# A fused two-layer adapter network on one core: the first round's mix and gates moved between the first adapter's folding and the others'

## The reference

```python
# layer 0: a 64x64 channel matrix per sample, then a dense product with a top-2 mixture of low-rank experts
y = jnp.einsum('bct,bcd->bdt', x, W_cond[condition])          # "mix"
base = jnp.einsum('bnd,od->bno', y, W_base) + b_base
top_p, top_i = jax.lax.top_k(softmax(y @ W_gate.T), 2)        # "gates", "routing"
h = jnp.einsum('bnd,erd->bner', y, A)                         # 8 experts of rank 16
x = x + base + einsum('bner,eor->bno', h * route_w, B)        # "delta"
# layer 1: each sample has one of 8 full matrices W1[adapter_ids], then low-rank heads
z = jnp.einsum('bsi,boi->bso', x, W1[adapter_ids])
scores = 8 * softmax(z @ Wr.T + br)
x = x + 2 * einsum('bshr,hor,bsh->bso', z @ A1, B1, scores)
```

## Time and profile before

| | value |
|---|---|
| median of three runs | 737.5 us |
| profiled execution | 738.8 us, of which its span is 737.1 us |
| TensorE (PE) busy | 719.6 us, 98% |
| weight loads (PEld) busy | 644.0 us, 87% |
| VectorE (DVE) busy | 335.2 us, 45% |
| ScalarE (ACT) busy | 114.0 us, 15% |
| GpSimd (POOL) busy | 58.0 us, 8% |
| moved by DMA | 156.24 MB, mean 212 GB/s |
| granted TensorE clock | 1.00 |

### The profile page before, as it was taken

How to read it: one execution, slowest core, us unless ns; L and a number is a source line. 1 busy time by engine, 2 the same in 40 slices (tenths; PEclk the granted TensorE clock), 3 DMA queues, 4 the chain that set the end, 5 groups by cost and what they waited for, 6 DMA issues and landing times.

```text
span 737.1 us, 12345 instructions
## 1 busy us (share of the span) xinstructions
PE 719.6 (98%) x4502; PEld 644.0 (87%) x4502; DVE 335.2 (45%) x887; ACT 114.0 (15%) x309; POOL 58.0 (8%) x115
## 2 busy tenths in 40 slices
PE   8999999999999999999999999999999999999996
PEld 8999887888888988898889888888889888988996
DVE  2000196235533654264534663464436543674644
ACT  2222300111111111112111111111111111120111
POOL 1222310000100010001000110001000100010100
PEclk9999999999999999999999999999999999999999
DMA  7899994145634775359526773387437751485552
GB/s 280 320 416 381 385 410 136 58 158 178 223 134 140 251 238 208 115 204 299 190 85 229 240 245 120 128 262 238 152 115 255 255 182 58 172 307 217 202 219 72
DMA packets 49457, 156.24 MB, mean 212 GB/s; under 512 B 8836, under 2 KB 26244, under 8 KB 39172
## 3 DMA queue, kind: packets, MB, share of 16 engines
q1 hardware_dynamic: 38466, 78.72, 30.0%
q0 software_dynamic: 9216, 71.31, 28.1%
q10 hardware_dynamic: 1730, 5.58, 1.9%
HBM read 133.24 MB, written 22.35 MB: 211 GB/s over the span
## 4 chain that ended last, share of the span: by engine, by line
PE 83%; issue 7%; DVE 5%; POOL 2%; DMA 2%; ACT 1%; POOLq 0%; ACTq 0%; DVEq 0%
PE base_ps L348 17%; PE base_ps L349 17%; PE base_ps L350 17%; PE mix_both L371 7%; PE out_ps L419 4%; PE low_ps L419 4%; PE mix_both L384 3%; DMA adapter<-folded 2%; POOL adapter L960 2%; PE base_ps L357 2%; PE out_ps L348 2%; PE out_ps L349 2%; PE out_ps L350 2%; DVE w_lo L700 1%; PE out_ps L384 1%
## 5 line engine op out<-in xcount | busy, mean ns | idle before, releaser
L348 PE MATMUL base_ps<-yT,w_hi 128*128 128x512 f32 (+1 forms) x576 | 214.7, 373 | 1.3 <-DVE xT L820 1.1
L350 PE MATMUL base_ps<-yT,w_hi 128*128 128x512 f32 (+1 forms) x576 | 211.4, 367 | 0.0
L349 PE MATMUL base_ps<-yT,w_lo 128*128 128x512 f32 (+1 forms) x576 | 211.4, 367 | 0.0
L704 DVE TENSOR_TENSOR yT<-mix_both,yT 128x512 fp32r<-128x512 f32 x64 | 44.3, 692 | 240.3 <-ACT yT L577 240.2
L348 PEld LDWEIGHTS base_ps<-yT,w_hi 128*128 128x128 f32 x576 | 108.5, 188 | 20.9 <-DVE xT L820 4.0
L350 PEld LDWEIGHTS base_ps<-yT,w_hi 128*128 128x128 f32 x576 | 108.4, 188 | 18.0
L349 PEld LDWEIGHTS base_ps<-yT,w_lo 128*128 128x128 f32 x576 | 108.6, 189 | 15.4
L357 PE MATMUL base_ps<-ag_raw,stage 128*128 128x136 f32 x640 | 75.2, 280 | 2.2 <-issue 1.2
L357 PEld LDWEIGHTS base_ps<-ag_raw,stage 128*128 128x128 f32 x640 | 74.5, 190 | 3.0 <-issue 2.3
L974 POOL DMA_DIRECT2D adapter<-folded x60 | 32.1, 534 | 568.7 <-PE low_ps L419 495.4
L716 DVE TENSOR_TENSOR x1T<-xT,x1T 128x256 fp32r<-128x256 f32 x120 | 45.4, 420 | 61.0 <-ACT x1T L584 61.0
(11 more groups left out here) (150 smaller groups left out, 740.8 us busy)
## 6 DMA issues: line engine op xcount, KB each, us to landing
adapter<-folded POOLq DMA_DIRECT2D x63, 1088.0 KB, 5.4
stage<-in_w SPq DMA_DIRECT2D x40, 512.0 KB, 7.9
x_rows<-in_x SPq DMA_DIRECT2D x32, 512.0 KB, 4.3
xT<-in_x_turned SPq DMA_DIRECT2D x16, 1024.0 KB, 6.3
out<-xT SPq DMA_DIRECT2D x28, 512.0 KB, 3.0
folded<-adapter ACTq DMA_DIRECT2D x10, 544.0 KB, 6.7
w_raw<-in_w SPq DMA_DIRECT2D x8, 256.0 KB, 7.7
w_raw<-in_w SPq DMA_DIRECT2D x4, 512.0 KB, 11.8
```

The source lines that it names most:

```text
L348: pe.matmul(dst, st_hi, mv_lo, start=start, stop=False, skip_group_check=True)
L349: pe.matmul(dst, st_lo, mv_hi, start=False, stop=False, skip_group_check=True)
L350: return pe.matmul(dst, st_hi, mv_hi, start=False, stop=stop, skip_group_check=True)
L704: dve.tensor_tensor(yT[:, 1, k, :], mix_ps[k % 2][:, :], yT[:, 0, k, :], ALU.subtract).then_inc(yT_lo_done, 1)
```

## The change

In the first round alone:

- **The mix's banks.** The mix uses four banks (`mix_ps[0]`, `mix_ps[1]`, `low_ps`, `out_ps`), and chunk k waits for the low half of chunk k-4. The gates' waits follow: tile 0 starts after five chunks, and from chunk 5 on, and for each further tile, there is a wait of its own.
- **Order on TensorE.** The mix and the gates stand between `fold(0)` and the loop of the other adapters. ScalarE's `yT_high` and its exponential, and VectorE's `copy_hg` and `routing`, move with them; on VectorE they now stand before the splits.
- **Order on SyncE.** x of round 0 and `g0` are loaded behind the first adapter's units and before the others'. The channel matrices of round 0 leave this queue.
- **GpSimd.** It issues the channel matrices of round 0, under a semaphore of their own, before `low_of_adapter(0)`, and splits g0 right behind `low_of_adapter(0)`.
- **The first unit** is loaded in two halves of 512 columns, each with its semaphore; the fold waits for the second half at its fifth piece.
- ScalarE's plain copy of a folded unit goes to `lg` and not to `hg`, since `hg` now holds the gates' sums of round 0 while other adapters are folded.

```diff
+        def mix_bank(q, r, k):
+            return hg_banks[k % 4] if isinstance(q, int) and r == 0 else mix_ps[k % 2]
...
             e = first_adapter(sp)
-            for c in range(KC):
+            piece = w1[bass.ds(KC * e, 1), :, :].rearrange("a p n -> (a p) n")
+            sp.dma_start(stage[:, 0, 0:T], piece[:, 0:T]).then_inc(first_landed, 16)
+            sp.dma_start(stage[:, 0, T:D], piece[:, T:D]).then_inc(unit_landed[0], 16)
+            for c in range(1, KC):
                 load_unit(e, c)
-            sp.wait_ge(const_set, 5)
             sp.wait_ge(small_landed, 48)
-            load_wc(0, 0)
             total = adapters_in_use(sp)
+            load_x(0, 0)
+            sp.dma_start(g_raw[:, :, 1, :], g0).then_inc(g_landed, 16)
             with sp.Fori(1, total) as n:
                 e = adapter_at(sp, n)
                 for c in range(KC):
                     sp.wait_ge(unit_done, KC * n + c + 1)
                     load_unit(e, c)
-            load_x(0, 0)
-            sp.dma_start(g_raw[:, :, 1, :], g0).then_inc(g_landed, 16)
...
                 for c in range(KC):
-                    pe.wait_ge(unit_landed[c], 16 * n + 16)
+                    if c == 0 and isinstance(n, int):
+                        pe.wait_ge(first_landed, 16)
+                    else:
+                        pe.wait_ge(unit_landed[c], 16 * n + 16)
                     pe.wait_ge(unit_copied, KC * n + c + 1)
                     for oc in range(KC):
+                        if c == 0 and oc == HALF and isinstance(n, int):
+                            pe.wait_ge(unit_landed[0], 16)
...
-                if k >= 2:
-                    pe.wait_ge(yT_lo_done, at(q, r, KC, k - 1))
+                banks = 4 if isinstance(q, int) and r == 0 else 2
+                if k >= banks:
+                    pe.wait_ge(yT_lo_done, at(q, r, KC, k - banks + 1))
...
-                        if t == 0 and k in (0, KC - 1):
+                        if t == 0 and isinstance(q, int) and r == 0:
+                            if k == 0 or k >= 5:
+                                pe.wait_ge(yT_lo_done, max(5, k + 1))
+                        elif t == 0 and k in (0, KC - 1):
...
+                        if t and k == 0 and isinstance(q, int) and r == 0:
+                            pe.wait_ge(yT_lo_done, 5 + t)
...
             fold(0)
+            for k in range(KC):
+                mix(0, 0, k)
+            pe.wait_ge(g_split, 1)
+            gates(0, 0)
             total = adapters_in_use(pe)
             with pe.Fori(1, total) as n:
                 fold(n)
             pe.wait_ge(unit_copied, KC * total + BANKS)
-            for k in range(KC):
-                mix(0, 0, k)
             iteration(0, 0, l1=False)
...
-                act.copy(hg[:, c % 4, :], base_ps[c % BANKS][:, 0:HG]).then_inc(unit_copied, 1)
+                act.copy(lg[:, c % 4, :], base_ps[c % BANKS][:, 0:HG]).then_inc(unit_copied, 1)
...
             take_adapter(0, e, False)
+            for k in range(KC):
+                yT_high(0, 0, k)
+            route_exp(0, 0)
             total = adapters_in_use(act)
...
             for k in range(KC):
                 yT_low(0, 0, k)
+            for t in range(TILES):
+                copy_hg(0, 0, t)
+            routing(0, 0)
             for k in range(KC):
                 split(w_hi[:, k, 0:T], w_lo[:, k, 0:T], w_raw[:, k, 0:T], w_landed[k], k)
...
+            pool.wait_ge(const_set, 5)
+            pool.wait_ge(small_landed, 48)
+            for i in range(PER):
+                no = pool.value_load(ids[0:1, i:i + 1], min_val=0, max_val=CONDS - 1)
+                half = slice((i % 2) * CH, (i % 2 + 1) * CH)
+                pool.dma_start(wc[half, i // 2, half], w_cond[bass.ds(no, 1), :, :].rearrange("a p n -> (a p) n")
+                               ).then_inc(first_wc_landed, 16)
             low_of_adapter(0)
+            pool.wait_ge(g_landed, 16)
+            pool.tensor_copy(g_hl[:, :, 0, :], g_raw[:, :, 1, :]).then_inc(g_split_hi, 1)
+            pool.wait_ge(g_split_hi, 1)
+            pool.tensor_tensor(g_hl[:, :, 1, :], g_raw[:, :, 1, :], g_hl[:, :, 0, :], ALU.subtract).then_inc(g_split, 1)
```

More of the change, by code:

```diff
@@ L154, in build @@
         ag1_landed = sem("ag1_landed")
+        first_landed = sem("first_landed")
         unit_landed = [sem(f"unit_landed{s}") for s in range(STAGE)]
@@ L173, in build @@
         wc_landed = sem("wc_landed")
+        first_wc_landed = sem("first_wc_landed")
         xT_landed = [sem(f"xT_landed{h}") for h in range(4)]
@@ L469, in iteration @@
                 first = isinstance(q, int) and r == 0
-                if first:
-                    pe.wait_ge(g_split, 1)
-                gates(q, r)
+                if not first:
+                    gates(q, r)
                 for k in range(KC):
@@ L576, in yT_high @@
                 act.wait_ge(yT_done, at(q, r, KC, k + 1))
-                act.copy(yT[:, 0, k, :], mix_ps[k % 2][:, :]).then_inc(yT_hi_done, 1)
+                act.copy(yT[:, 0, k, :], mix_bank(q, r, k)[:, :]).then_inc(yT_hi_done, 1)
             def x1T_high(q, r, i):
@@ L597, in lwT_high, with route_exp @@
                 act.copy(lwT[:, 0, toks], low_ps[:, toks]).then_inc(lwT_hi_done, 1)
+            def route_exp(q, r):
+                act.wait_ge(route_step, at(q, r, ROUTE_STEPS, 6))
+                act.activation(top_exp[:, :, :], top_d[:, :, :], ACT.Exp).then_inc(top_exp_done, 1)
             def iteration(q, r, l1=True, ahead=True):
@@ L602, in iteration @@
                     x1T_high(q, r - 1, 1)
-                act.wait_ge(route_step, at(q, r, ROUTE_STEPS, 6))
-                act.activation(top_exp[:, :, :], top_d[:, :, :], ACT.Exp).then_inc(top_exp_done, 1)
-                if l1:
+                    route_exp(q, r)
                     for i in range(2, PER):
@@ L626, in _ @@
                 take_adapter(n, e, True)
-            for k in range(KC):
-                yT_high(0, 0, k)
             iteration(0, 0, l1=False)
@@ L703, in yT_low @@
                 dve.wait_ge(yT_hi_done, at(q, r, KC, k + 1))
-                dve.tensor_tensor(yT[:, 1, k, :], mix_ps[k % 2][:, :], yT[:, 0, k, :], ALU.subtract
+                dve.tensor_tensor(yT[:, 1, k, :], mix_bank(q, r, k)[:, :], yT[:, 0, k, :], ALU.subtract
                                   ).then_inc(yT_lo_done, 1)
@@ L861, in iteration @@
             def iteration(q, r, l1=True, ahead=True, toks=ALL):
-                copy_hg(q, r, 0)
                 if l1:
+                    copy_hg(q, r, 0)
                     x1T_low(q, r - 1, 0)
-                copy_hg(q, r, 1)
-                if l1:
+                    copy_hg(q, r, 1)
                     x1T_low(q, r - 1, 1)
[L868 to L871, removed]
+                    copy_hg(q, r, 2)
+                    copy_hg(q, r, 3)
+                    routing(q, r)
                     for i in range(2, PER):
@@ L959, in low_of_adapter @@
                     pool.wait_ge(unit_copied, KC * n + c + 1 + BANKS)
-                    pool.tensor_tensor(adapter[:, 0, c, 1, :], hg[:, c % 4, :], adapter[:, 0, c, 0, :], ALU.subtract
+                    pool.tensor_tensor(adapter[:, 0, c, 1, :], lg[:, c % 4, :], adapter[:, 0, c, 0, :], ALU.subtract
                                        ).then_inc(folded_lo, 1)
+            pool.wait_ge(const_set, 5)
[5 more added lines that the diff above has]
+                               ).then_inc(first_wc_landed, 16)
             low_of_adapter(0)
+            pool.wait_ge(g_landed, 16)
+            pool.tensor_copy(g_hl[:, :, 0, :], g_raw[:, :, 1, :]).then_inc(g_split_hi, 1)
+            pool.wait_ge(g_split_hi, 1)
+            pool.tensor_tensor(g_hl[:, :, 1, :], g_raw[:, :, 1, :], g_hl[:, :, 0, :], ALU.subtract).then_inc(g_split, 1)
             total = adapters_in_use(pool)
```

10 lines of the change are left out of this document (4 added, 6 removed).

## The result

The changed kernel is slower by 0.5%: 741.86 us, median of 8 runs (740.01 to 743.27), against 738.27 us in 8 runs of the kernel before. The ratio is 1.0047, 95% interval 1.0036 to 1.0058. The forecast was 731.0, with 736.5 as its upper end. The profiled execution has a span of 741.2 us where before had 737.1.

A forecast was written before the change was run, and what follows sets the result against it. TensorE bounds the kernel, so only its idle time can be gained: base starts 5.2 us earlier and the 1.29 us routing wait goes, 6.5 us off the 737.5 median, giving 731.0 us; range 729.8 to 736.5.

The forecast's parts named there:

- The rival: Second round's channel matrices: SyncE's queue behaves as now, TensorE waits 11.6 us, 742.6 us in all; chance 0.10 (738 to 743).
- 40.3 us of queue against 28.7: From folds' end to second round's mix: matrices now take 40.3 us to arrive, the changed kernel wants them after 28.7.
- 27.2 us behind the folds' end: Second round's matrices: the queue shrinks, they land at 124.2 with folds ending at 97.0, 1.5 us before they are wanted.
- without b1 in front the first block of 11.5 us falls away: SyncE's issues of x's columns: the first blocked issue, 11.5 us, was held until b1 left the queue, so it goes.
- The margin: Second round's matrices land 1.5 us before wanted; chance of partly late 0.14 (732 to 736), of queue as now 0.10.
- The wait before the first mix: TensorE after the first fold: ready at 22.3, x lands at 22.8, so 0.5 us of wait, bounds 0 and 1.7.
- The first piece in two: Start of the first fold: half a unit lands earlier, 0.6 us gained, bounds 0 and 0.8; second unit may limit next.
- bound by loads: Rival in the fold loop: loads limit it, gain shrinks to 1 or 2 us, 736; chance 0.08 for little change.
- the 1.98 and the 1.29 us: TensorE idle before: 1.98 us at the second adapter's start, 1.29 us waiting for the routed rows; both were to go.
- hidden as put: First round's matrices on GpSimd's queue: landing near 20, hidden by the first fold, cost 0; upper bound 4.4 us.
- 97.6 predicted: Start of base on TensorE: 97.6 and not 102.9, 5.2 us gained.
- GpSimd beside VectorE's splits: Low parts of the last two adapters slow to 1.6 us at most against a unit's 1.85; folding keeps its pace.

## Why the prediction was wrong, point by point

**The rival had the mechanism, the forecast had the wrong size.** The text (731.0 us) put 40.3 us of queue against 28.7, and then let the queue shrink to 27.2 us behind the folds' end. It took 35.1 (folds' end 101.14, the mix started 136.25). Term by term: the store landed 6.6 us after its issue and not 5.0 (1.6). From its landing to the end of the last columns' issue were 15.6 us (109.0 to 124.63) and not 8.7 (6.9). The rest was 11.6 and not 12.3. **The step that failed is "without b1 in front the first block of 11.5 us falls away".** It became 7.0, and the second stayed at 5.9 us. b1 may have been a reason for the length of the first block, but it isn't one for there being a block. In the changed kernel b1 had landed by 109.5, no DMA was under way when the two x_turned were issued (the row below, in the order of the table by stretches), and still the third issue of columns stood from 111.65 to 118.66.

```profile
109.00:110.00 1.00, 1.00 (x7) 1.00 0.00 0
```

By the kernel with x as rows it is the number of pieces in the queue that counts. The row of b1's landing at 105.6 lay near the release at 106.3, and that was read as its cause; the rows of the second block (released at 112.3, with nothing of b1 left) spoke against it and were already in the earlier trace rows. The rival's 742.6 us lies near the measured 741.86 in part by luck: it had 6.5 us gained and 11.6 waited, and in the profiled executions it was 2.5 gained, 6.6 waited, 1.5 of half clock, and 1.6 us given back behind that.

**The margin.** By the text the matrices were 1.5 us early in a sum of five terms with bounds of several us. The chance for their being late, partly or in full, was 0.24. With such a margin, and with the demand 28.7 and no longer 48.0 us behind the folds' end, that was low. It also named the price as the wait alone, and left out the half clock behind a long wait, 1.5 us here.

**x.** The wait before the first mix was put at 0.5 and was 2.3, above its bound of 1.7. The start of the count was wrong. The last unit of the first adapter landed 10.6 us after its issue, at 18.2 and not at 16.4: the 9.3 us of the earlier trace rows are the median of two, of which the later one landed at 17.0 already in the kernel before, and DMA moved only 272 GB/s from 6 to 9 us in the changed kernel, where it had moved 393. From there x took 7.0 us and not 6.4, at 390 GB/s (8 to 24 us) and not at 0.41 MB/us. The kernel with the stores late confirms the bytes' share. The half clock behind this wait (1.7 us in the profiled execution) was in no term.

**The first piece in two.** The half landed after 3.2 us and the fold started at 6.70, 1.4 us earlier, more than put. The second unit then stood in its way for 0.9 us, as feared, and x's wait ate the rest: no gain. That the halves come with a slower DMA from 6 to 9 us was in no term.

**What was right.** Without a stall the mix took 7.2 us; the gates 7.7; the folds came at their old pace (59.5 us for 32 units with the loop's entry), so they didn't become bound by loads; the 1.98 and the 1.29 us are gone. GpSimd issued the first round's matrices from 6.92 to 15.4 us and they landed 5.2 to 5.7 us later, hidden as put. Most of what base's start was to gain, it gained once x came earlier: 98.53 in the kernel with late stores, with 1.0 us of wait left, against 97.6 predicted.

**GpSimd beside VectorE's splits.** The Trainium skill (GPSIMD Engine Reference, Key points) names contention between the two engines when a VectorE instruction is in a two-port mode or has two inputs from SBUF, as the subtraction of a split has. The changed kernel's rows agree: GpSimd's subtraction takes 0.47 us elsewhere, and 0.74 to 0.95 in three of the five that stand beside splits. In the other two it takes 0.47, and the split beside it is longer (0.73 for 0.42 us, 0.95 for 0.69). It didn't slow the folds.

```profile
92.51 0.47 POOL L988 TENSOR_TENSOR adapter<-lg,adapter 128x136 fp32r<-128x136 f32 x1 [1.37 <-ACT lg L588]
94.29 0.74 POOL L988 TENSOR_TENSOR adapter<-lg,adapter 128x136 fp32r<-128x136 f32 x1 [1.31 <-ACT lg L588]
...
98.07 0.95 POOL L988 TENSOR_TENSOR adapter<-lg,adapter 128x136 fp32r<-128x136 f32 x1 [1.00 <-ACT lg L588]
```

## What to carry to other kernels

When work is moved forward out of a place, ask what the place had hidden: here some 19 us of mix (10.4), gates (7.6) and wait (1.3) had covered a chain of transfers that begins at the folds' end and ends, eight issues later, in the next round. Compute that chain's length against the new distance, and if the margin is smaller than its terms' bounds, move the chain too; one reordering in the queue made this kernel 6.8 us faster. A queue that holds its issuer back is read from the length of the issues. In this case small transfers that TensorE waits for did best in front of large scattered ones, or on another queue.

## What the runs showed of the hardware that was not expected

- SyncE's issue of a transfer can be held back for many us by what was issued before, and the number of pieces counts: 4 x 512 pieces of 1 KB behind two x_turned transfers were issued in 14.7 us, the same bytes in 4 x 128 pieces in 2.5 us. Eight 64-piece issues behind g0's 1024 pieces took 18.6 us, and 9.3 behind the columns in the changed kernel or behind the rows.
- A wait of 2.2 to 2.4 us in TensorE was followed by 1.2 GHz for some 3.5 us in the profiled executions of the changed kernel, of the one with the matrices early and of the one with two banks (0.79 from 24 to 32 us), and by no change of clock in that of the kernel with x as rows (2.27 us, 1.00). What decides it these runs don't show.
- Loading the first unit in two halves came with 257 to 325 GB/s from 6 to 9 us in all nine kernels that do so, against 393 to 411 in the five that load it in one transfer.
